# Head rows of the stacked q and k: sixteen rows in a block instead of every third row, copies ordered by half

## What is computed

```python
q = split(x @ W_q.T)      # 16 heads of 16 channels
k = split(x @ W_k.T)
v = split(x @ W_v.T)
attn = softmax(scale * einsum('bnqd,bnkd->bnqk', q, k), axis=-1)
o = einsum('bnqk,bnkd->bnqd', attn, v)
return o @ W_o.T
```

## Time and profile before

| what | value |
|---|---|
| median of three runs | 1072.7 us |
| the profiled execution: its own time | 1072.7 us |
| its span | 1070.9 us |
| TensorE matmul busy | 1007.7 us, 94% |
| VectorE busy | 757.5 us, 71% |
| ScalarE busy | 537.0 us, 50% |
| GpSimd busy | 271.4 us, 25% |
| chain that ended last, TensorE's share | 82% |

### The profile page before, as it was taken

One profiled execution on the slowest core, in us unless ns is written; L12 is line 12 of the kernel. 1 busy time (PEld: TensorE's weight loads), 2 busy tenths in 40 slices (PEclk: granted clock), 3 DMA queues, 4 the chain that ended last, 5 costly groups with the idle time before them and its releaser, 6 DMA issues.

```text
span 1070.9 us, 17165 instructions
## 1 busy us (share of the span) xinstructions
PE 1007.7 (94%) x5416; PEld 621.9 (58%) x5416; DVE 757.5 (71%) x1208; ACT 537.0 (50%) x1119; POOL 271.4 (25%) x260
## 2 busy tenths in 40 slices
PE   5999999996999999999999999999999999999768
PEld 4777777774444455645654564565456455545656
DVE  5788788995766887677687767867775786686232
ACT  4466555453554655456455545645563554456221
POOL 1265422221000322222122213212321321122133
PEclk9899999996999999989989998999999899999979
DMA  9445564442320330313033021303121230300000
GB/s 286 121 108 139 138 147 120 119 99 65 109 61 2 85 90 2 80 50 65 10 94 80 9 77 52 65 11 92 55 37 52 58 65 3 84 31 1 25 0 21
DMA packets 93685, 75.11 MB, mean 70 GB/s; under 512 B 44848, under 2 KB 79736, under 8 KB 93632
## 3 DMA queue, kind: packets, MB, share of 16 engines
q1 hardware_dynamic: 79040, 57.20, 20.2%
q10 hardware_dynamic: 14592, 17.25, 6.8%
HBM read 27.73 MB, written 12.61 MB: 38 GB/s over the span
## 4 chain that ended last, share of the span: by engine, by line
PE 82%; DVE 11%; issue 3%; DMA 2%; ACT 1%; SPq 1%; POOL 0%; DVEq 0%; POOLq 0%; ACTq 0%
PE bank L1091 19%; PE bank L358 12%; PE bank L943 11%; PE bank L924 11%; PE bank L1135 9%; PE raw_pair L883 6%; PE bank L809 3%; DVE rowmax L891 3%; PE bank L859 2%; PE bank L1210 2%; PE bank L1004 2%; DVE amax L440 2%; PE bank L381 2%; PE bank L1060 1%; DVE h L410 1%
## 5 line engine op out<-in xcount | busy, mean ns | idle before, releaser
L891 DVE TENSOR_REDUCE rowmax<-raw_pair 128x2 f32<-128x1024 f32 x256 | 313.0, 1223 | 131.4 <-PE raw_pair L883 131.4
L932 ACT ACTIVATE probs<-bank 128x512 f32<-128x512 f32 x512 | 280.9, 596 | 238.1 <-PE bank L924 236.3
L883 PE MATMUL raw_pair<-k_stack,q_stack 48*128 48x512 f32 x512 | 180.8, 471 | 20.2 <-DVE rowmax L891 19.7
L358 PE MATMUL bank<-up_w,xs_part 128*128 128x512 f32 x768 | 194.8, 407 | 5.2 <-issue 3.7
L924 PE MATMUL bank<-q_stack,k_stack 50*128 50x512 f32 x512 | 197.6, 459 | 1.4 <-issue 1.1
L358 PEld LDWEIGHTS bank<-up_w,xs_part 128*128 128x128 f32 x768 | 144.2, 193 | 40.7 <-issue 7.1
L943 PE MATMUL bank<-probs,v_ext 128*17 128x512 f32 x1024 | 141.4, 625 | 0.3
L1121 POOL TENSOR_TENSOR hid<-scratch,hid 128x512 fp32r<-128x512 f32 x64 | 82.4, 1288 | 220.6 <-ACT hid L1117 220.6
L924 PEld LDWEIGHTS bank<-q_stack,k_stack 50*128 50x128 f32 x512 | 81.9, 192 | 80.4 <-issue 56.5
L1091 PE MATMUL bank<-xf_part,gate_w 128*128 128x512 f32 x384 | 107.1, 415 | 4.9 <-POOL xf_part L1081 4.1
L1091 PEld LDWEIGHTS bank<-xf_part,gate_w 128*128 128x128 f32 x384 | 68.0, 190 | 67.2 <-issue 50.8
(11 more groups left out here) (121 smaller groups left out, 1117.9 us busy)
## 6 DMA issues: line engine op xcount, KB each, us to landing
q_stack<-split SPq DMA_DIRECT2D x48, 128.0 KB, 2.9
q_stack<-hid SPq DMA_DIRECT2D x48, 128.0 KB, 2.9
xk<-xT SPq DMA_DIRECT2D x32, 128.0 KB, 3.0
xt<-x_tok SPq DMA_DIRECT2D x32, 128.0 KB, 2.7
x_spill<-x1t ACTq DMA_DIRECT2D x32, 128.0 KB, 2.6
xa_spill<-xa ACTq DMA_DIRECT2D x32, 128.0 KB, 2.3
x_in<-xa_spill SPq DMA_DIRECT2D x8, 512.0 KB, 4.2
k_stack<-split ACTq DMA_DIRECT2D x32, 128.0 KB, 4.8
```

Of the source, the lines that this page charges most:

```text
L358: last = nc.tensor.matmul(bank[j][:], xs_part[a][:, m % 2, k, :], up_w[w][:, k, col + j * W:col + (j + 1) * W], start=(i == 0), stop=(i == ...
L883: mm = nc.tensor.matmul(raw_pair[:, half, :], q_stack[rows, slot, qt * P:(qt + 1) * P], k_stack[rows, slot, :], start=True, stop=True)
L891: nc.vector.reduce_max(rowmax[:, e:e + RAWS + 1:RAWS], raw_pair[:], AX.X).then_inc(raw_read, 1)
L932: nc.scalar.activation(probs[:, (kt % 2) * J + j, :], score_bank[c % 3][:], ACT.Exp).then_inc(exp_done, 1)
```

## The change

The partitions of a destination change. Before, part r of a head wrote every third partition of the 48, beginning at r (r, r + 3, ..., r + 45). Now it writes the sixteen neighbouring partitions 16 r to 16 r + 15. It is the same in `q_stack` and `k_stack`, so that the products in the contraction are the same in another order. And SP's six copies of q go half by half (half 0: r = 0, 1, 2; then half 1) where they went part by part (r = 0 in both halves, r = 1 in both, r = 2 in both). The count, the size and the source of the copies stay, and so do the waits.

```diff
         def stack_dma(eng, m, w, half, r):

             part = ((0, 0, 1), (0, 1, 0))[w][r]
-            eng.dma_start((q_stack, k_stack)[w][64 * half + r:64 * half + ROWS:ROWS // HD, G * m:G * m + G, :]
+            eng.dma_start((q_stack, k_stack)[w][64 * half + HD * r:64 * half + HD * (r + 1), G * m:G * m + G, :]
                           .bitcast(f32), staging(m, w)[part][64 * half:64 * half + 64, :].bitcast(f32)) \
                 .then_inc(stacked[m], 16)
...
-                for r in rows:
-                    for half in range(2):
+                for half in range(2):
+                    for r in rows:
                         stack_dma(sp, m, w, half, r)
```

## The result

The changed kernel took 1101.7 us (median of four runs, 1098.31 to 1105.64) against 1071.35 us for the kernel before on the same chip: a ratio of 1.0286, 95% interval 1.024 to 1.0333. The forecast was 1081, the range 1064 to 1113. The profiled execution of the changed kernel took 1097.92 us with a span of 1096.1, 25.2 us over the span before.

What follows compares the result with a forecast made beforehand. TensorE, busy 94% of the span, was taken as the bound, with the copies only just off its path. Batch 0 2.5, batch 1 0.8, batches 2 to 7 2.4, m = 0 0.3, clock 1.7: 7.7 us, forecast 1081, range 1064 to 1113.

Steps and rivals of the forecast that it cites:

- forecast case: Stack copies before the raw matmuls: twelve copies at 138 GB/s land 2.5 us later, costing 7.7 us; chance 0.44.
- serial rival: Stack copies go one after another at 110 GB/s, landing 5.4 us later, costing 40 us (1113); chance 0.22.
- if TensorE waited over 3 us: Sign at the raw matmuls that the forecast case is wrong and the serial rival holds.
- Where the margin is: Last landing before half step 5's raw matmul: 0.0 to about 0.6 us of room; m = 0 has 2.2 to 4.3.
- The rate: Twelve stack copies: 138 GB/s throughout, taking 11.4 us instead of 8.9.
- L: Delay of the last stack copy's landing, forecast at +2.5 us, with bounds of -1 and +10.
- The cover at half step 6: An existing 1.37 us wait for VectorE's maximum hides a delay up to 2.1 us in batch 2, 1.7 in batch 1.
- margins of 0.0, 0.1 and 0.6 us: Room between last landing and half step 5's raw work, in batches 0, 1 and 2; later batches repeat batch 2.
- the same sum: Whole kernel: batch 0 2.5, batch 1 0.8, batches 2 to 7 2.4, m = 0 0.3, clock 1.7; 7.7 us.
- The clock: TensorE in batch 0: the new wait brings one 3.41 us stretch at half clock, costing 1.7 us.
- the two that the prediction allowed: Sign on TensorE's clock: wrong if the stretches at 0.50 change in number by more than two.
- The clock rival: At half steps 5 and 6 the split lull keeps TensorE's clock up, some nine stretches gone, giving 1063; chance 0.12.

Runs made afterwards that it cites:

- e2: Rows in blocks of 16 neighbours, SP's copies in the old order, against the kernel before: 1100.81 us, ratio 1.0298.
- e3: Every third row as before, only SP's q copies going half by half, against the kernel before: 1069.42 us, ratio 0.9998.
- e7: The kernel before, with ScalarE issuing its k copies of m = 1 one half step later: 1073.73 us, ratio 1.0036.
- 0-15 with 16-31: Group in a copies-only kernel without the computation: four 256 KB copies, into partitions 0-15 and 16-31 in turn: 123 GB/s.

## Why the prediction was right in kind and short in size

The loss was forecast at 8 us and is 30. The path, the wait and its place were right. The measured 1101.7 us is beyond the 1095 up to which the forecast case was carried; it is inside the range only because that reaches to the serial rival. By the prediction's own sign the forecast case is wrong as well: it was to be dropped for the serial one if TensorE waited over 3 us, and its eight waits at half step 5 are 3.0 to 3.4 us on the matmuls. (A slip: 1080.4 was given as 1081.)

**Where the margin is.** Right. The wait came at half step 5 in each of eight batches, and at half step 21 of batch 0 alone (1.7 us). SP's issue times stayed.

**The rate.** This is the mis-sized term. The prediction took 138 GB/s, of two every-third copies into one half, and so L = 2.5. The twelve copies went at 126 GB/s in batch 2: 12.5 us in place of 11.4, and with the 0.6 us outside the transfers L was 4.2. The row was of the wrong kind: a copy into every third row has three rows on its fullest path, one into neighbours has four. The two edits were given one answer; the rows have all of the loss and the order none that can be measured (e2, e3). The 104 GB/s that the prediction quotes from the Trainium skill (SBUF — State Buffer, section "Door 1: The DMA port swizzle") erred to the other side, with an estimated L of 6.

**The cover at half step 6.** Right, and borne out by e3 and e7, where L of 1.2 and 1.8 cost nothing measurable and 3.8 us; without a cover the latter would cost about 11 (1.8 less the margins of 0.0, 0.1 and 0.6 us, over eight batches), and its interval ends at 6.5. With L = 4.2 put into the same sum: 4.2 in batch 0, 2.5 in batch 1, 2.1 in six batches, 2.0 for m = 0 in batch 0, 1.7 for the clock, together 23.0 us. The spans differ by 25.2.

**The clock.** One stretch at half clock was counted, in batch 0. The changed kernel has three there, of 3.4 us each, where the kernel before has none: two from the wait of half step 5 on and one behind that of half step 21. The two waits and the windows of these stretches; then the first q copies of batches 0 and 1, of the changed kernel and of the kernel before:

```profile
280.62 0.80 PE L882 MATMUL raw_pair<-k_stack,q_stack 48*128 48x512 f32 x2 [3.04 <-DMA k_stack<-hid]
323.09 0.51 PE L882 MATMUL raw_pair<-k_stack,q_stack 48*128 48x512 f32 x2 [1.41 <-DMA k_stack<-split]
...
279.70:286.50 6.80, 5.88 (x17) 2.97 (x21) 1.81 (x2) 2.18 (x4) 0.00 (x0) 0.51 0.29 94
324.10:327.50 3.40, 3.40 (x15) 1.10 (x13) 2.06 (x2) 1.54 (x3) 0.00 (x0) 0.53 0.02 3
...
265.76 3.84 SPq L829 DMA_DIRECT2D q_stack<-hid  x6
...
354.13 3.80 SPq L829 DMA_DIRECT2D q_stack<-hid  x6
...
268.68 3.82 SPq L830 DMA_DIRECT2D q_stack<-hid  x6
...
347.96 3.81 SPq L830 DMA_DIRECT2D q_stack<-hid  x6
```

Two stretches more than counted, at 1.7 us of work each, are 3.4 us. From the six q copies of batch 0 to those of batch 1 are 354.13 - 265.76 = 88.4 us, against 79.3 in the kernel before (268.68 to 347.96): 9.1 us, more than any other batch loses. The two waits of 3.0 and 1.4 us and three stretches at 1.7 us come to 9.5. In batch 2 the fall comes right behind the wait: the projection before half step 6 takes 2.9 us where it took 1.66, and half step 6's raw matmul starts 7.4 us behind half step 5's score where it was 4.1. But that is the batch's only stretch at half clock where there were two, and from its first q copy to the next batch's it loses 1.8 us (97.35 against 95.57). The other batches lose 1.5 to 4.1.

Counted in windows of 3.41 us over the whole span, batches 1 to 7 have 13 stretches at half clock before and 13 after: there they only moved. The whole span has 26 where it had 25, three more in batch 0 and two fewer in phase 1, and so stays within the two that the prediction allowed. In phase 1, which the change hardly touches, the profiled execution of before had 6.8 us at half clock, whose row is below, that the one of after hasn't, and the one of after reached the first q copies of m = 1 2.9 us sooner. That makes the profiled difference of 25.2 us smaller than the 28.1 that was lost from these copies on. The medians differ by 30; the sum at L = 4.2 with three stretches in place of one gives 26.4, so that 2 to 4 us are not accounted for.

```profile
36.20:43.00 6.80, 6.80 (x18) 4.16 (x16) 3.83 (x10) 2.17 (x7) 1.63 (x3) 0.50 0.56 135
```

**The rivals.** The serial one was nearest in mechanism: 0-15 with 16-31 at 123 GB/s shows that copies into neighbours gain little from lying on different paths, but they go at 116 to 126 GB/s, not 110. Its L of 5.4 and its 40 us were too much, as 2.5 and 8 were too little. The clock rival did not come: L was too large for it, and where L was right for it (e3, e7) the medians show no gain. The profiled execution of e3 had a mean clock of 0.977 against 0.960, but that is one execution, and the ten timed runs of e3 are even with before.

## What to carry to other kernels

The copies into 16 partitions inside SBUF went by the fullest path that they write: with a step of 2 or 4 at 197 and 198 GB/s, with a step of 3 at 132, as neighbours at 116. So lay such rows out with a step of 2 or 4 where you can. Whether it matters was here a question of the due time (3.6 us for the copies with room, 26 for those without), so put the landing of the last copy beside the start of its first reader, batch by batch, and count what the reader waits for next as cover. As for the clock, look whether the new wait comes where TensorE ran without a lull: in batch 0 three stretches at half clock followed, 5.1 us, but in the seven batches that had such stretches already their number stayed the same.
